# Cross-attention and a mixture of experts on one core: four dense expert pieces moved ahead of the gathered tiles, attended rows kept per batch element

## The chip, the cores and the metric

The kernel runs on one core of one Trainium2 chip. A core has TensorE (PE in the profile; PEld is its weight load), VectorE (DVE), ScalarE (ACT), GpSimd (POOL) and SyncE (SP), which issues most of the DMAs. The metric is the device time of one execution in microseconds (us).

## What is computed

```python
x = x + attn(layernorm(x), ctx, Wq, Wk, Wv, Wo)     # x (32, 56, 512), ctx (32, 1500, 512)
    # 16 query heads, 4 key/value heads of 96; keys and values from ctx and the normed x
x = x + ffn(layernorm(x), W_gate, b_gate, W_e, b_e)
    # logits = x @ W_gate + b_gate; the top 2 of 8 experts for each row
    # y_e = relu(x @ W_e + b_e); the mean of the two chosen y_e
```

There are 32 batch elements of 56 rows, so 1792 rows, which make 14 tiles of 128. Everything is float32; each product is made of three passes with operands split in a high and a low part (TERMS), so each operand is first copied ("hi") and then subtracted ("lo").

## The kernel before

Four blocks of code follow one another, `project`, `attend`, `combine` and `experts`. Each is a `with nc.Block()` with one program per engine, and at its end all engines meet: no engine begins the next block until all have ended this one.

**attend** (L538 on) loops over the 32 elements. For each one SP brings the unnormalized attended rows back, POOL divides them, and `store_att` writes them to `scratch["att"]`, a DRAM tensor of (1536 head rows, 1792 token rows): 1536 pieces of 224 bytes for an element. The rows of the first tile are read back and split by POOL at the end of this block (`first`, L650 to L654).

**combine** (L1008 on) makes the output projection, tile by tile (`output(t, parts)`, L1295: 36 matmuls of 512 columns into one bank). Tile t's attended rows are loaded by SP with `load_rows` (1536 pieces of 512 bytes), two tiles ahead, split by ACT (L1180, hi) and DVE (L1207, lo). DVE adds x and normalizes (`norm`, L926 to L938; it waits until the normed rows of the tile before have been stored, since they use one buffer), SP stores x1 and the normed rows (`store_rows`), PE turns them over (`turn`, L1279, halfway through the next tile's matmuls) and makes the logits (`logits`, L953), DVE picks the top two (`choose`), PE ranks them (`rank`), DVE finds each token's place (`put`), and POOL scatters the token numbers to `scratch["ids"]` (`scatter`, L1161, two indirect DMAs of a tile). The first 12 tiles (OS) are routed in this way: their tokens are gathered into 31 tiles (NT) by expert. The last two tiles (OD) are dense: all eight experts are computed for all their rows and weighed with 0 or a half (16 pieces, STEPS). POOL meanwhile splits the early part of the expert weights (L1149, L1154). At the end of the loop SP loads the late part of the weights of experts 0 to 3 (`load_late`, L978), then the bias (L1098, 2 MB), waits for the last scatter, loads `id_table` (L1103), and issues the late loads 4 and 5, each when POOL has split the buffer's former tenant (L1004).

**experts** (L1330 on): PE turns the id table (L1580, L1581), DVE makes the row indices (L1483 to L1489), POOL gathers rows of `scratch["xn"]` with an indirect DMA for a tile (L1434; three buffers, XRING), PE turns each (L1560), ACT and DVE split it (L1456, L1497), and PE multiplies it with its expert (`product`, L1573, 15 matmuls, banks in a ring of three). DVE adds the bias (`evict`, L1502), ACT applies the relu (L1471; L1478 with the weights of a dense piece), POOL writes the result back (`put_back`, L1424). Then come the logits of the dense tiles and the 16 dense pieces; POOL adds pieces to their rows of x1 (L1446, L1447, `summed`), and DVE closes the routed tiles in between:

```python
                    if i >= LAG and i - LAG < OS:
                        close(i - LAG)            # LAG = 3: tiles 0 to 11 behind pieces 3 to 14
```

`close(t)` (L1515, L1517) adds the two expert rows of each token, which SP has loaded with `load_y` (L1380, three buffers; the next is issued when `close` has freed one), and SP stores the tile (L1383).

Of the kernel before, what the change touches and what calls it, by code (L numbers as in the profile page):

```python
# [31 lines left out]
P = 128  # L32
# [4 lines left out]
E = 8  # L37
# [70 lines left out]

PIECES = ((0, 0, 0, 0, D), (1, 0, D, 0, D), (2, 0, 2 * D, 0, D // 2), (2, 1, 0, D // 2, D), (3, 1, D // 2, 0, D))
# [103 lines left out]
def load_rows(sp, scratch, t, att, loaded):  # L213

    sp.dma_start(att, scratch["att"].rearrange("(k p) r -> p k r", p=P)[:, :, bass.ds(t * P, P)]).then_inc(loaded, 16)
# [275 lines left out]
def attend(nc, w, stream, io, scratch):  # L491


    with ExitStack() as ctx:
# [20 lines left out]
        first = f(w["wv"][0][:]).rearrange("p k c -> p (k c)").rearrange("p (k r) -> p k r", r=P)  # L515
# [22 lines left out]
        with nc.Block() as block:  # L538
            @block.sync
            def _(sp):  # L540
# [64 lines left out]
                load_rows(sp, scratch, 0, first, first_loaded)  # L605
# [8 lines left out]
            def _(pool):  # L614
# [30 lines left out]
                for n in range(LOADS - 1):  # L645
                    split_wo(pool, stream, n)
                    if n == RAW - 1:
                        (hi, lo), third = stream["first_parts"], HT // 3
                        pool.wait_ge(first_loaded, 16)
                        pool.tensor_scalar(hi, first, 1.0, 0.0, ALU.mult, ALU.add).then_inc(stream["first_hi"], 1)  # L650
                        pool.wait_ge(stream["first_hi"], 1)
                        for i in range(3):
                            k = slice(i * third, (i + 1) * third)
                            op = pool.tensor_tensor(lo[:, k], first[:, k], f(hi[:, k]), ALU.subtract)  # L654
                        op.then_inc(stream["first_lo"], 1)
# [262 lines left out]
def norm(dve, g, t):  # L918
# [16 lines left out]
    dve.wait_ge(g["turned"], START + min(t, OS))  # L935
# [21 lines left out]
def choose(dve, g, t, sel):  # L957
# [13 lines left out]
    dve.wait_ge(g["sel_ready"], 2 * t + 2)  # L971

# [35 lines left out]
def combine(nc, stream, g, io, scratch):  # L1008

    with ExitStack() as ctx:  # L1010
# [15 lines left out]
        att = [stream["rows"], sb("att", [P, HT, P])[:]]  # L1026
        ats = [[home, sb(f"att_{n}", [P, HT, P], F32R)[:]] for home, n in zip(stream["first_parts"], ("hi", "lo"))]
        w_raw = g["area"][:, 0:2 * EARLY_W].rearrange("p (n c) -> p n c", n=2)
        home = [g["area"][0:HD, 2 * EARLY_W + i * H * Q:2 * EARLY_W + (i + 1) * H * Q] for i in range(2)]
# [6 lines left out]
        loaded = [sem(f"rows_loaded{i}") for i in range(2)]  # L1036
# [11 lines left out]

        with nc.Block() as block:
            @block.sync  # L1050
            def _(sp):
                def load(t):
                    load_rows(sp, scratch, t, att[t % 2], loaded[t % 2])
# [10 lines left out]
                load(1)  # L1064
# [11 lines left out]
                for t in range(OT):  # L1076
                    if t + 2 < OT:
# [4 lines left out]
                        if t + 2 == OT - 1:  # L1082
                            sp.wait_ge(stream["att_stored"], START + B * 16)
                        load(t + 2)
# [6 lines left out]
                    if t == OT - 2:  # L1091

                        sp.wait_ge(a_lo, START + OT - 2)
                        for e in range(LATE_RING):
                            load_late(sp, g, io, e)

                        sp.wait_ge(g["e_lo"], E)
                        sp.dma_start(g["area"][:, 0:E * D], io["be"].broadcast_to([P, E * D])).then_inc(g["bias_loaded"], 16)  # L1098
# [76 lines left out]
            def _(act):  # L1175
                def split(t):
                    act.wait_ge(loaded[t % 2], (t + t % 2) // 2 * 16)
# [14 lines left out]
                for t in range(OT - 1):  # L1192
# [3 lines left out]
                    if t < OS:  # L1196
                        turn(t)
# [4 lines left out]
            def _(dve):  # L1202
                for s in (a_lo, g["logits_ready"]):
                    dve.sem_inc(s, START)
                def split(t):
                    dve.wait_ge(a_hi, t + 1)
                    dve.tensor_tensor(ats[1][t % 2], att[t % 2], f(ats[0][t % 2]), ALU.subtract).then_inc(a_lo, 1)  # L1207
# [58 lines left out]
                find_tiles()  # L1266
                split_late_lo(dve, g, POOL_LATE)

            @block.tensor
            def _(pe):  # L1270
# [18 lines left out]
                def output(t, parts):  # L1289

                    n = 3 * HT
                    for j in range(n):
# [8 lines left out]
                        if 0 < t <= OS and j == n // 2:  # L1301
# [7 lines left out]
                    mm.then_inc(o_done, 1)  # L1309

# [19 lines left out]
def experts(nc, stream, g, io, scratch, out_d):  # L1330

    with ExitStack() as ctx:
# [15 lines left out]
        sel, half = sb("selected_dense", [P, 2, E]), sb("halves", [P, OD, E])  # L1348
# [8 lines left out]
        turned, x_hi, x_lo = sem("turned_e"), sem("xs_hi_ready"), sem("xs_lo_ready")  # L1357
# [4 lines left out]
        joined, chosen, summed = sem("joined"), sem("chosen"), sem("summed")  # L1362
# [4 lines left out]
        NV, STEPS = NT + OD, OD * E  # L1367

        with nc.Block() as block:
            @block.sync  # L1370
            def _(sp):
# [27 lines left out]
                for s in range(XRING):  # L1399
                    sp.wait_ge(y_stored[s], 16 * len(range(s, NT, XRING)))  # L1400
# [20 lines left out]
            def _(pool):  # L1421
                def put_back(j):
                    pool.wait_ge(relu_done, j + 1)
                    pool.indirect_dma_start(out=scratch["y"], out_offset=bass.IndirectOffsetOnAxis(y_row[:, j:j + 1], 0),  # L1424
                                            in_=y[:, j % XRING], in_offset=None).then_inc(y_stored[j % XRING], 16)
# [14 lines left out]

                for i in range(STEPS - 1):
                    s, rows = (NT + i) % XRING, x1[:, i // E]
                    pool.wait_ge(relu_done, NT + i + 1)
                    if i > 0:
                        pool.wait_ge(summed, i)
                    pool.tensor_tensor(rows[:, 0:D // 2], rows[:, 0:D // 2], y[:, s, 0:D // 2], ALU.add)  # L1446
# [261 lines left out]
```

## Time and profile before

| what | value |
|---|---|
| median of the runs (3 runs, 3391.44 to 3392.01) | 3391.51 us |
| the profiled execution's own time | 3390.29 us |
| its span (first to last instruction) | 3388.4 us |
| PE busy | 3341.6 us (99%) |
| DVE, ACT, POOL busy | 2052.6, 1648.8, 1051.4 us (61%, 49%, 31%) |
| mean granted TensorE clock | 0.994 |

The times of rows are microseconds from the start of the span; "mean ns" is that of one instruction. In a view of windows each engine has its busy time with the number of its instructions in brackets, then come the granted clock of TensorE (1.00 is 2.4 GHz, 0.50 is 1.2 GHz), the mean busy share of the 16 DMA engines, and GB/s. A q behind an engine's name means its sequencer; idle time stands behind an instruction in square brackets with what ended it. Matmuls overlap, so the starts of two neighbours, not the duration of one, give the pace.

### The profile page before, as it was taken

The numbers are of one execution on the slowest core, as the hardware profiler recorded it, in microseconds if no ns is written. First come the engines' busy times: TensorE is split into PE (matmuls) and PEld (weight loads), VectorE is DVE, ScalarE is ACT, GpSimd is POOL, SyncE is SP. The second block draws the span as 40 slices with busy tenths as digits, with TensorE's granted clock in tenths as the row PEclk, the third lists the DMA queues.
The fourth block names the chain that finished last, engine by engine and source line by source line (L and its number), as shares of the span: only waits on it lengthen the run. The fifth ranks groups of instructions, "written<-read, shape, count | busy, mean of one in ns | idle before, by whom it ended". The sixth has DMA issues, their size and how long they took to land. (4 is left out here: it accounts for less than half of the span.)

```text
span 3388.4 us, 64330 instructions
## 1 busy us (share of the span) xinstructions
PE 3341.6 (99%) x21610; PEld 3107.7 (92%) x21610; DVE 2052.6 (61%) x2995; ACT 1648.8 (49%) x3146; POOL 1051.4 (31%) x865
## 2 busy tenths in 40 slices
PE   8999999999999999999999999999999999998989
PEld 8989999999999999999999999999999999997777
DVE  5346666666666666666666666666666666665645
ACT  3225555555555555555555555555555555552232
POOL 0032223332333333332222222233323333326554
PEclk9999999999999999999999999999999999999989
DMA  6542222222212122222222222222222121226865
GB/s 229 198 144 59 59 65 65 65 61 61 63 46 60 56 63 65 64 65 64 65 65 59 65 57 60 65 65 65 61 61 61 47 61 55 63 75 164 195 194 188
DMA packets 307512, 282.96 MB, mean 84 GB/s; under 512 B 200634, under 2 KB 257546, under 8 KB 307338
## 3 DMA queue, kind: packets, MB, share of 16 engines
q1 hardware_dynamic: 301738, 266.10, 27.6%
q0 software_dynamic: 5728, 16.27, 1.5%
q8 instruction: 26, 0.43, 0.1%
q14 instruction: 20, 0.16, 0.0%
HBM read 208.33 MB, written 73.96 MB: 83 GB/s over the span
## 5 line engine op out<-in xcount | busy, mean ns | idle before, releaser
L822 PE MATMUL ps_proj<-wv_hi,parts 128*125 128x384 f32 x3072 | 875.6, 339 | 0.0
L767 DVE TENSOR_TENSOR probs_lo<-probs,probs_hi 125x448 fp32r<-125x448 f32 (+1 forms) x896 | 682.0, 778 | 275.7 <-ACT probs_hi L694 263.2
L809 PE MATMUL ps_proj<-parts,wk_hi 128*128 128x500 f32 x2304 | 711.1, 390 | 2.9 <-DVEq L722 2.9
L822 PEld LDWEIGHTS ps_proj<-wv_hi,parts 128*125 128x125 f32 x3072 | 560.0, 185 | 5.8
L147 POOL TENSOR_SCALAR parts<-raw 128x1000 fp32r<-128x1000 f32 (+1 forms) x198 | 238.3, 1204 | 957.2 <-PE ps_proj L822 777.8
L686 ACT ACTIVATE probs<-ps_scores 125x448 f32<-125x448 f32 (+1 forms) x896 | 463.0, 517 | 121.6 <-PE ps_scores L870 78.8
L822 PE MATMUL ps_proj<-wv_lo,parts 128*125 128x384 f32 x1536 | 518.4, 338 | 0.0
L809 PEld LDWEIGHTS ps_proj<-parts,wk_hi 128*128 128x128 f32 x2304 | 431.4, 188 | 91.6 <-DVEq L722 3.2
L673 ACT CAST values_hi<-ps_proj 125x384 fp32r<-125x384 f32 x384 | 184.4, 480 | 645.3 <-PE ps_proj L822 645.3
L694 ACT CAST probs_hi<-probs 125x448 fp32r<-125x448 f32 (+1 forms) x896 | 484.1, 540 | 28.3
L736 DVE TENSOR_TENSOR values_lo<-ps_proj,values_hi 125x384 fp32r<-125x384 f32 x384 | 214.3, 558 | 431.6 <-ACT values_hi L673 428.9
L870 PE MATMUL ps_scores<-queries_hi,keys_lo 104*125 104x224 f32 (+1 forms) x1664 | 454.6, 273 | 0.0
L865 PE MATMUL ps_scores<-queries_hi,keys_hi 96*125 96x224 f32 (+1 forms) x1664 | 452.3, 272 | 0.0
L866 PE MATMUL ps_scores<-queries_lo,keys_hi 96*125 96x224 f32 (+1 forms) x1664 | 451.8, 272 | 0.0
L888 PE MATMUL ps_attended<-probs_hi,values_hi 125*97 125x224 f32 x1664 | 447.5, 269 | 2.0 <-DVE probs_lo L767 1.6
L809 PE MATMUL ps_proj<-parts,wk_lo 128*128 128x500 f32 x1152 | 448.5, 389 | 0.0
L889 PE MATMUL ps_attended<-probs_hi,values_lo 125*96 125x224 f32 x1664 | 442.6, 266 | 0.0
L890 PE MATMUL ps_attended<-probs_lo,values_hi 125*97 125x224 f32 x1664 | 442.3, 266 | 0.0
L202 POOL TENSOR_TENSOR probs<-probs 96x448 f32<-96x448 f32 x31 | 35.7, 1152 | 1209.7 <-DMA probs<-inverse_sums 1209.7
L667 ACT CAST keys_hi<-ps_proj 96x500 fp32r<-96x500 f32 x288 | 164.9, 573 | 501.6 <-PE ps_proj L809 501.6
L727 DVE TENSOR_TENSOR keys_lo<-ps_proj,keys_hi 96x500 fp32r<-96x500 f32 x288 | 192.8, 670 | 336.6 <-ACT keys_hi L667 336.2
L870 PEld LDWEIGHTS ps_scores<-queries_hi,keys_lo 104*125 104x125 f32 (+1 forms) x1664 | 306.5, 184 | 2.3
(218 smaller groups left out, 5822.7 us busy)
## 6 DMA issues: line engine op xcount, KB each, us to landing
raw<-in_ctx SPq DMA_DIRECT2D x192, 500.0 KB, 3.6
qk_hi<-proj_out_hi SPq DMA_DIRECT2D x60, 224.0 KB, 2.0
qk_lo<-proj_out_lo SPq DMA_DIRECT2D x60, 224.0 KB, 2.4
queries_hi<-qk_hi SPq DMA_DIRECT2D x32, 336.0 KB, 3.5
queries_lo<-qk_lo SPq DMA_DIRECT2D x32, 336.0 KB, 3.6
att_raw<-attended SPq DMA_DIRECT2D x128, 84.0 KB
probs<-att_raw SPq DMA_DIRECT2D x31, 336.0 KB, 5.7
probs<-inverse_sums SPq DMA_DIRECT2D x31, 336.0 KB, 3.0
```

The source lines that it names most:

```text
L147: pool.tensor_scalar(hi, raw, 1.0, 0.0, ALU.mult, ALU.add).then_inc(stream["hi"], 1)
L686: act.activation(pr[0:R, u % PRING, 0:N], psc[0:R, u % SBANKS, 0:N], ACT.Exp, scale=SCALE).then_inc(exp_done, 1)
L694: act.copy(prs[0][0:R, u % PRING, 0:N], pr[0:R, u % PRING, 0:N]).then_inc(p_hi, 1)
L767: dve.tensor_tensor(prs[1][0:R, u % PRING, 0:N], pr[0:R, u % PRING, 0:N], f(prs[0][0:R, u % PRING, 0:N]), ALU.subtract).then_inc(p_lo, 1)
L809: mm = pe.matmul(pproj[n % 2][:, 0:CS], w["wk"][a][:, j // 3, i * P:(i + 1) * P], ct[v][:, c, j // 3, :], start=(j == 0), stop=(j == 3 * K ...
L822: mm = pe.matmul(pproj[n % 2][0:VT, 0:KD], ct[a][:, t // VTC, j // 3, s], w["wv"][v][:, j // 3, :], start=(j == 0), stop=(j == 3 * KT - 1))
L865: pe.matmul(o, kt[0][:, h, s], q[0][0:HD, c], start=True, stop=False)
L866: pe.matmul(o, kt[0][:, h, s], q[1][:, c], start=False, stop=False)
L870: mm = pe.matmul(o, kt[1][:, h, s], q[0][:, c], start=False, stop=True)
L888: pe.matmul(o, vt_hi[:, t, h], hi, start=(t == 0), stop=False)
L889: pe.matmul(pav[0:HD, h % 2, 0:GQ], vt_lo[:, t, h], hi, start=False, stop=False)
L890: mm = pe.matmul(o, vt_hi[:, t, h], lo, start=False, stop=(t == NVT))
```

## The change

It does two things, and moves steps that hang on them.

**Attended rows per element.** `scratch["att"]` becomes (32, 96, 896): `store_att` writes an element as it is, and `load_element` reads one as 128 runs of 2688 bytes. A ring of six element buffers (ERING) takes the place of two tile buffers; the rows of Wo are put in the matching order before the launch. Since 128 is no multiple of 56, a tile's split becomes one instruction for each of the three or four elements that it touches (`segments`), on ACT, DVE and, for the first tile, POOL. The late weight loads now wait for the split of the last tile, and the bias load goes in front of them.

**Four dense pieces first.** The first dense tile (12) is turned in tile 13's matmuls, at five sixths, and its logits follow the last matmul of combine; ACT and DVE split it into slot 2 of `xs`, and `shares` makes its weights, all in combine. In experts PE begins with pieces 0 to 3 of that tile; the id table is turned (`find_rows`) behind piece 0, the first gathered tile in front of piece 3. ACT's and DVE's splits of the late weights 4 to 7 are interleaved with the relu (`weigh`) and eviction of these pieces. POOL adds the four pieces (`gather_dense`) between the gathers of tiles 2 and 3. Twelve dense pieces remain behind the gathered tiles, and the 12 closes are spread over pieces 3 to 11 of them.

```diff
-    sp.dma_start(scratch["att"].rearrange("(h d) (b q) -> b d h q", d=HD, q=Q)[b],
-                 home[0].rearrange("d (h q) -> d h q", q=Q)).then_inc(stream["att_stored"], 16)
+    sp.dma_start(scratch["att"][b], home[0]).then_inc(stream["att_stored"], 16)
...
+def load_element(sp, scratch, e, home, loaded):
+    rows = scratch["att"][e].rearrange("d c -> (d c)").rearrange("(p c) -> p c", p=P)
+    sp.dma_start(home, rows).then_inc(loaded, 16)
...
+                        for e in range(ERING + 2, B):
+                            if last_tile(e - ERING) == t:
...
+                                load(e)
...
-                        sp.wait_ge(a_lo, START + OT - 2)
+                        sp.wait_ge(g["e_lo"], E)
+                        sp.dma_start(g["area"][:, 0:E * D], io["be"].broadcast_to([P, E * D])).then_inc(g["bias_loaded"], 16)
+
+                        sp.wait_ge(a_lo, START + OT - 1)
                         for e in range(LATE_RING):
                             load_late(sp, g, io, e)
...
-                    act.copy(ats[0][t % 2], att[t % 2]).then_inc(a_hi, 1)
+                    for e, q, n, c in segments(t):
+                        op = act.copy(ats[0][t % 2][:, :, c:c + n], rows_of(t, e, q, n))
+                    op.then_inc(a_hi, 1)
...
-                        if 0 < t <= OS and j == n // 2:
+                        if 0 < t and j == (n // 2 if t <= OS else 5 * n // 6):
                             turn(t - 1)
...
+                    if t == OT - 1:
+                        logits(pe, g, OS)
...
+                    if j == XRING - 1:
+                        for n in range(FIRST):
+                            gather_dense(n)
...
+                pe.wait_ge(x_lo, 1)
+                for n in range(FIRST):
+                    late_lo_done(pe, g, n)
+                    if n == FIRST - 1:
+                        turn(0)
+                    product(n, FIRST_SLOT, slice(n, n + 1))
+                    if n == 0:
+                        find_rows()
+                turn(1)
...
-                    if i >= LAG and i - LAG < OS:
-                        close(i - LAG)
+                    for t in range(closed, OS * max(i - LAG + 1, 0) // (LAST - LAG)):
+                        close(t)
+                        closed += 1
```

## Rows read from the trace of the kernel before

**Rows 1.** Windows of four stretches: us, busy by engine, clock, DMA share, GB/s.

```profile
155.00:3062.90 2907.90, 2903.01 (x19335) 2727.91 (x19333) 1803.54 (x2483) 1516.09 (x2931) 874.42 (x667) 1.00 0.23 65
3062.90:3215.50 152.60, 142.37 (x674) 115.69 (x673) 93.38 (x244) 33.33 (x44) 87.80 (x99) 0.96 0.82 192
3232.80:3238.30 5.50, 5.39 (x18) 4.51 (x18) 2.88 (x6) 0.88 (x2) 0.94 (x1) 0.53 0.43 139
3232.80:3382.50 149.70, 149.52 (x846) 127.93 (x845) 75.51 (x125) 47.02 (x81) 81.65 (x88) 0.98 0.59 194
```

**Rows 2.** Waits of TensorE over the whole span: us in total, times, longest.

```profile
PE ps_table L1580 <- DMA id_table<-token_ids: 8.6, 1, 8.6
PE ps_t L1279 <- DVE xn_g L938: 7.6, 4, 4.9
PE ps_t L1560 <- DMA x_gathered<-xn_rows,index: 5.9, 2, 5.6
```

**Rows 3.** The end of the combine block, line 1049: duration ns, start us.

```profile
L1049 SPq DRAIN  x1: 122/122/122, 3223.1 to 3223.1; - x1
...
L1049 PEldq EVENT_SEMAPHORE  x1: 51/51/51, 3223.3 to 3223.3; - x1
```

**Rows 4.** The subtractions of the late weights: duration ns min/median/max, start us.

```profile
L1004 POOL TENSOR_TENSOR parts<-raw,parts x3: 1817/1847/1854, 3211.1 to 3214.8; 128x768 fp32r<-128x768 f32 x3
```

**Rows 5.** DMA packets in 3118 to 3120 us and in 3224 to 3226 us.

```profile
DMA packets 1118, 0.62 MB, mean 312 GB/s; under 512 B 13, under 2 KB 1082, under 8 KB 1118
...
DMA packets 273, 0.75 MB, mean 373 GB/s; under 512 B 30, under 2 KB 30, under 8 KB 273
```

**Rows 6.** TensorE in order of time, behind its longest wait in this stage.

```profile
3117.03 1.12 PE L1279 MATMUL ps_t<-ident_g,xn_g 128*128 128x128 f32 x4 [4.93 <-DVE xn_g L938]
```

**Rows 7.** The chain of work that ended last: start us, us, what.

```profile
3209.81 11.98 DMA token_ids<-token_ids_f,places
...
3223.93 0.64 PE ps_table L1580 x2
...
3226.24 1.01 POOL x_gathered L1434
...
3227.56 4.10 DMA x_gathered<-xn_rows,index
...
3232.93 5.33 PE ps_e L1573 x15
3238.26 0.44 PE ps_t L1560 x4
3238.69 2.79 PE ps_o L1573 x15
...
3335.69 0.79 PE ps_g L953 x8
...
3382.54 0.70 DVE y L1502
...
3384.02 0.69 DVE x L1548
```

**Rows 8.** Groups by line, 3330 to 3389 us: busy us, mean ns.

```profile
L1446 POOL TENSOR_TENSOR x<-x,y 128x256 f32<-128x256 f32 x15 | 15.2, 1010 | 19.3 <-ACT y L1478 19.3
...
L1478 ACT ACTIVATE y<-y,halves 128x512 f32<-128x512 f32 x16 | 11.6, 724 | 34.6 <-DVE y L1502 34.6
L1447 POOL TENSOR_TENSOR x<-x,y 128x256 f32<-128x256 f32 x15 | 11.0, 734 | 0.0
...
L1517 DVE TENSOR_TENSOR raw<-raw,x_gathered 128x512 f32<-128x512 f32 x6 | 4.2, 692 | 0.2
```

**Rows 9.** DMA issues from 3040 us on: count, KB each, us to landing.

```profile
x_gathered<-expert_rows SPq DMA_DIRECT2D x8, 512.0 KB, 4.9
...
out<-raw SPq DMA_DIRECT2D x9, 256.0 KB, 4.7
raw_then_bias<-in_be SPq DMA_DIRECT2D x1, 2048.0 KB, 18.2
```

More of the change, by code:

```diff
@@ L604, in _ @@
                 sp.wait_ge(att_stored, START + (B - 1) * 16)
-                load_rows(sp, scratch, 0, first, first_loaded)
+                for e, *_ in segments(0):
+                    load_element(sp, scratch, e, first[e], first_loaded)
                 load_wo(sp, stream, io, RAW)
@@ L933, in norm @@
     dve.wait_ge(g["rstd_done"], t + 1)
[L935 removed]
+    dve.wait_ge(g["turned"], START + t)
     if t > 0:
@@ L1034, in combine @@
         pcnt = g["ptab"][:, 0:E]
-        loaded = [sem(f"rows_loaded{i}") for i in range(2)]
+        loaded, fourth_loaded = [sem(f"element_loaded{i}") for i in range(ERING)], sem("fourth_loaded")
         small_loaded, consts = g["small_loaded"], sem("consts_g")
@@ L1051, in _, with load @@
             def _(sp):
-                def load(t):
-                    load_rows(sp, scratch, t, att[t % 2], loaded[t % 2])
+                def load(e):
+                    load_element(sp, scratch, e, slots[e % ERING], loaded[e % ERING])
                 def load_x(t):
@@ L1195, in _ @@
                         split(t + 2)
-                    if t < OS:
-                        turn(t)
+                    turn(t)
+                act.copy(g["xs"][0][:, FIRST_SLOT], pt[:]).then_inc(g["x_hi"], 1)
                 for e in range(LATE_RING):
@@ L1367, in experts @@
         NV, STEPS = NT + OD, OD * E
+        LAST = STEPS - FIRST
+        dense = [(n // E, n % E) for n in range(STEPS)]
+        step = lambda n: n if n < FIRST else NT + n
+        stored = lambda s, j: 16 * len([i for i in range(j) if (FIRST + i) % XRING == s])
         with nc.Block() as block:
@@ L1439, in _ @@
                     put_back(j)
[L1441 to L1446, printed above, removed]
-                    pool.tensor_tensor(rows[:, D // 2:], rows[:, D // 2:], y[:, s, D // 2:], ALU.add).then_inc(summed, 1)
+                for n in range(FIRST, STEPS - 1):
+                    gather_dense(n)
             @block.scalar
@@ L1502, in evict, with evict_dense @@
                     dve.tensor_tensor(y[:, s], po[s][:], which, ALU.add).then_inc(biased, 1)
-                def gate(d):
-                    choose(dve, g, OS + d, sel)
-                    dve.tensor_tensor(half[:, d], sel[:, 0], sel[:, 1], ALU.add).then_inc(joined, 1)
-                    dve.wait_ge(joined, d + 1)
-                    dve.tensor_scalar(half[:, d], half[:, d], 0.5, None, ALU.mult).then_inc(chosen, 1)
+                def evict_dense(n):
+                    i = step(n)
+                    if i >= FIRST + NT and i - XRING < FIRST + NT:
+                        dve.wait_ge(y_stored[i % XRING], stored(i % XRING, NT))
+                    elif n >= XRING:
+                        dve.wait_ge(summed, n - XRING + 1)
+                    evict(i, bias[:, dense[n][1]])
                 def close(t):
@@ L1589, in _ @@
                     e = pe.value_load(expert_i[0:1, j:j + 1], min_val=0, max_val=E - 1)
-                    product(j, j, bass.ds(e, 1))
+                    pe.wait_ge(x_lo, j + 2)
+                    product(FIRST + j, j % XRING, bass.ds(e, 1))
                     if j + 2 < NV:
                         turn(j + 2)
-                logits(pe, g, OS)
-                for i in range(STEPS):
-                    product(NT + i, NT + i // E, slice(i % E, i % E + 1))
-                    if i == 0:
+                for n in range(FIRST, STEPS):
+                    v = NT + dense[n][0]
+                    pe.wait_ge(x_lo, v + 2)
+                    product(step(n), v % XRING, slice(dense[n][1], dense[n][1] + 1))
+                    if n == FIRST:
                         logits(pe, g, OS + 1)
```

208 lines of the change are left out of this document (129 added, 79 removed).

## The prediction

> **What bounds the kernel now.** I read the windows first. In attend TensorE is busy for 2903.0 of 2907.9 us at the full clock, with the DMA engines at 0.23 of their time [rows 1]: nothing that the change does to a store there can shorten it. So everything happens in the last 326 us. Combine takes 152.6 us for 142.4 us of TensorE work, with the DMAs at 0.82; experts is full from 3232.8 us on. The waits of TensorE name what is left: 7.6 us in four waits for the normed rows, 8.6 us for the id table and 5.9 us for the gathered rows [rows 2]. The last two are one hole between the blocks. The chain says how it comes about: the last scatter takes 11.98 us to land, then the id table is loaded and turned at 3223.93 us, POOL starts a gather at 3226.24 us, its rows come with the transfer that begins at 3227.56 us and takes 4.10 us, and the first product runs 5.33 us where the next takes 2.79 us [rows 7], because the clock stands at 0.53, near the 1.2 GHz level, over that stretch [rows 1].
>
> One row decides how much of this hole four dense pieces can fill: SP leaves combine at 3223.1 us, and TensorE is let into the next block at 3223.3 us [rows 3]. The pieces stand in experts, behind that meeting. They can't use the time from 3215.5 us on, only what comes after 3223.4 us.
>
> **The middle, step by step (before's clock times, combine unchanged so far).** TensorE comes out of 8 us of idleness, so piece 0 is a slow product: 5.33 us [rows 7], 3223.5 to 3228.8 us. Only then is the id table turned. From that turn to POOL's first gather before were 2.3 us (3223.93 to 3226.24), and from there to the rows 5.4 us (3226.24 to 3231.66) [rows 7]. Now: gather begins at about 3231.2 us, rows by 3236.6 us at the latest. Meanwhile TensorE does pieces 1 and 2 at 2.8 us each, to about 3235.3 us, and wants to turn gathered tile 0. The wait is between 0 and 1.3 us; the 5.4 us are those of a gather with another behind it, so I take 0.5 us. Piece 3 and a turn (2.8 and 0.44 us) bring it to 3239.5 us. The splits of tile 0 stand on ACT and DVE behind the relu and eviction of piece 2, each step some 0.7 us [rows 7, 8], and come out near 3239.7 us. I let the first gathered product begin at 3240.0 us.
>
> Before, 46 products, 31 turns and two logits stood behind 3238.26 us and took 144.2 us, to 3382.45 us. Now 43 products, 31 turns and one logits stand behind 3240.0 us: 144.2 - 3 x 2.80 - 0.79 = 135.0 us [rows 7], so 3375.0 us.
>
> **A new wait behind POOL.** The four additions are queued in front of gather 3. Piece 3 ends near 3239.1 us; evicted (0.7), weighed (0.72) and added (1.01 + 0.73) [rows 7, 8], with the splits of tiles 0 and 1 in the same two queues (about 1 us more), POOL is free at 3243.3 us. Gather 3 lands 4.1 to 5.4 us later, 3247.4 to 3248.7 us. TensorE has finished two gathered products and a turn at 3246.0 us. It waits 1.4 to 2.7 us; I take 2.0. Later gathers have three products of lead and catch up. TensorE would then end at 3377.0 us, 5.4 us earlier than before.
>
> **The meeting itself moves a little.** The bias (2 MB, landing after 18.2 us behind the first late weights [rows 9]) now stands in front of those weights, and they wait for tile 13's split as well. The bytes are the same and start at the same point, so the last of them lands near 3222 us as before, but this is now a weight: ACT has to copy it and DVE or POOL to subtract, 1.84 us on POOL [rows 4], which ends near 3224 us. The scatter, which no longer has the bias behind it but small pieces, may come sooner; that doesn't help when the weights are last. Bounds 0 and 3.6 us (if the weights came only behind all 18.2 us of the bias); I take 0.9 us, since the total of bytes decides. The turn of tile 12 (0.44 us) and the logits (0.79 us) moved into combine end at some 3217 us and hide in the same hole.
>
> **The tail gets longer.** Before, the last close is done while the last piece runs: TensorE ends at 3382.45, eviction at 3382.54, the last addition at 3384.02 to 3384.71 us [rows 7], 2.3 us behind TensorE. Now 12 closes stand behind 9 pieces, two of them behind the last eviction. That alone is 2 x 1.4 us. But the loads of the pairs bind too: the buffer of close t is refilled for close t + 3, with 4.9 us to landing [rows 9] and up to 0.5 us for SP, which also waits at t = 1, 2 and 3 for a store of 4.7 us [rows 9] in front of the next load. I laid the steps out with e3, the end of piece 3 of the twelve, as zero and 2.81 us a piece: close 3 ends at 9.2, close 7 at 19.6, close 8 at 21.7, close 9 at 23.8, close 10 at 26.2, close 11 (its load issued at 21.8 behind close 8) at 28.3, and the last addition at 29.0 us. TensorE has ended at 22.5 us. So 6.5 us stand behind TensorE in place of 2.3 us: 4.2 us lost, and TensorE isn't held up, since eviction 9 is late but only a thirteenth piece would need its bank. Bounds: 1.3 us (loads never late) and about 8 us (landing a us later).
>
> **Combine.** Bytes stay the same, packets change. 13 loads of 1536 runs of 512 bytes become runs of 2688 bytes. In a stretch that is nearly all 512-byte packets the engines moved 312 GB/s, in one with large ones 373 GB/s [rows 5]. A tile of 0.79 MB is 2.5 us against 2.1 us. With the last element's store (1536 pieces of 224 bytes) some 6 to 7 us of DMA time go, out of 0.82 x 152.6 = 125 us. The normed rows queue behind these loads, and TensorE's four waits are waits for such a store, one of 4.9 us and three that share 2.7 us [rows 2]. If each store comes 1 to 2 us sooner, those three go and the long one keeps about 3 us: 4.5 us gained. The bounds are 0 and 7.6 us plus what the clock costs after the long wait: four transposes behind it took 1.12 us where four take 0.44 us [rows 6, 7], and if the slow stretch costs what it costs the first product (5.33 - 2.79 us), it is 10 us. I take 4.5 us. On the cost side the splits become three or four instructions. ACT is busy 33 of 152.6 us and DVE 93 of 152.6 us [rows 1]; at a few tenths more for a tile this is hidden by the 10.9 us of a tile (152.6 / 14), and would cost those tenths x 13, 5 us, if DVE were the bound.
>
> The Trainium skill, "DMA: Bandwidth & Descriptors", section Specifications, puts the smallest transfer at line rate at 512 bytes. By that rule the 13 loads gain nothing and only the 224-byte store does, and the sum would be that of the first rival below. The two stretches of this trace differ by a fifth and so speak against it, but one of them is mixed.
>
> **The sum.** Middle -5.4, meeting +0.9, tail +4.2, combine -4.5: -4.8 us. Against the profiled execution's 3390.3 us that is 3385.5 us; the median of the runs is 1.2 us above that execution, so 3386.7 us. 0.2% is 6.8 us here, about what a measurement of this kernel tells from no change.
>
> **The rivals.**
> - Packets don't matter in combine (the waits stay as they are): -0.3 us, 3391.2 us. For it: TensorE's longest wait follows the scatters, and those stay. Against: the DMAs stand at 0.82, so small savings come out larger in the queue. Chance 0.15.
> - The DMA relief clears combine: all four waits and the slow clock go, -10 us there, -10.3 us in all, 3381.2 us; with a tail at its lower bound 3378.3 us. For it: three of the four waits share 2.7 us. Chance 0.35.
> - Slower: the pair loads bind the tail. The stretch behind the gathered tiles already runs the DMAs near their limit, and 12 closes must now fit between fewer pieces. Each us by which the landing of a pair exceeds 4.9 us is paid at every third close, some 3.5 us in all. At 6.3 us the kernel is as before, from 8.2 us on it is slower by 0.2%; at 8.5 us it is 3399 us. Against: 4.9 us was measured in the very same traffic. Chance 0.07.
> - My forecast, 3384 to 3391 us: 0.43.
>
> **Chances and range.** Faster by over 0.2% (under 3384.7 us): the clearing rival and a little of my own case, 0.38. Slower: 0.07. Within 0.2%: 0.55. The range goes from 3377.5 us, the second rival with a short tail, to 3396 us, the unknown costs (meeting 3.6, tail 8) without any gain in combine.
>
> **What the profile of the changed kernel would show.** The meeting 15 to 16 us behind tile 12's last matmul; the first product behind it at half clock and 5.3 us long; the id table turned behind it; a wait of 1 to 3 us in front of the turn of gathered tile 3, released by a gather; 43 products from there without a gap; two closes and an addition behind the last eviction, with DVE waiting for loads of pairs. In combine the longest wait for the normed rows at about 3 us. I would be wrong if combine's waits grew or vanished, if the meeting moved by more than 2 us against combine's matmuls, or if the last addition stood within 3 us of TensorE's end.

## The result, and the profile after

The changed kernel takes 3404.57 us (median of 6 runs, 3398.91 to 3408.93), the kernel before, timed beside it, 3393.54 us (6 runs, 3391.44 to 3396.39). The ratio is 1.003, with a 95% interval of 1.0018 to 1.0041: slower by 0.3%, 11.0 us. The prediction said 3386.7 us and gave this side 0.07. The profiled execution took 3398.9 us, the shortest of the six, with a span of 3397.2 us.

Windows of the changed kernel over the same kinds of stretches as [rows 1]: attend, combine up to its last product, from there to the meeting, from the meeting to TensorE's end, and behind it. The columns are those of [rows 1].

```profile
155.00:3063.60 2908.60, 2901.44 (x19330) 2727.41 (x19328) 1802.75 (x2483) 1514.31 (x2931) 874.17 (x669) 1.00 0.22 65
3063.60:3217.40 153.80, 144.00 (x685) 117.25 (x685) 97.92 (x273) 33.93 (x69) 78.31 (x96) 0.95 0.83 191
3217.40:3233.10 15.70, 0.04 (x1) 0.00 (x0) 2.97 (x10) 3.32 (x4) 6.04 (x3) 0.57 0.63 166
3233.10:3386.20 153.10, 150.26 (x849) 127.96 (x849) 75.74 (x118) 48.68 (x84) 83.85 (x88) 0.99 0.56 182
3386.20:3394.60 8.40, 0.03 (x1) 0.00 (x0) 7.52 (x11) 1.94 (x3) 3.72 (x4) 0.75 0.86 330
```

Read the first column: attend is as before. In the profile of before, the meeting behind attend ended at 3064.4 us (the window of [rows 1] begins 1.5 us earlier) and combine's products at 3215.4 us, 151.0 us behind it; the meeting let TensorE go on 7.9 us later, TensorE ended 159.1 us behind the meeting and the last addition 2.3 us behind that. Now it is 153.8, 15.7, 153.1 and 8.4 us. One stretch of four is shorter, by 6.0 us; the other three are longer, by 2.8, 7.8 and 6.1 us. The stretch of 153.8 us ends with tile 12's logits, which stood in experts before; they and that tile's turn are 1.2 us of the 2.8 (0.79 and 0.44 us by the prediction's rows).

The waits of TensorE from combine on, to set against [rows 2]:

```profile
PE ps_e L1654 <- PEq L1086: 15.9, 1, 15.9
PE ps_t L1333 <- DVE xn_g L959: 8.4, 3, 7.6
PE ps_t L1642 <- DMA x_gathered<-xn_rows,index: 1.2, 1, 1.2
PE ps_o L1654 <- DVE wk_lo L1570: 1.2, 1, 1.2
```

The id table and the gathered rows are gone from the list, as intended, but the first row is a new wait of 15.9 us for the end of the block itself, and the wait for the normed rows has grown to 7.6 us in one piece. The two waits of 1.2 us are new too: one for the fourth gathered tile, one for the split of the first. The long wait stands at the same place as in [rows 6], and the four transposes behind it again run at half clock (granted 0.50 from 3115 to 3120 us). DVE, which makes the normed rows, had itself waited 9.29 us for the store of the tile before. SP had issued that store at 3100.92 us, so it took 17.3 us:

```profile
3118.82 1.11 PE L1333 MATMUL ps_t<-ident_g,xn_g 128*128 128x128 f32 x4 [7.61 <-DVE xn_g L959]
3118.22 0.55 DVE L959 TENSOR_SCALAR xn_g<-x,mv_g,rstd_g 128x512 f32<-128x512 f32 x1 [9.29 <-DMA xn_rows<-xn_g]
```

The end of the combine block (line 1086, against [rows 3]), the late weights' subtractions (against [rows 4]) and the first copy of them on ACT:

```profile
L1086 POOLq DRAIN  x1: 6237/6237/6237, 3226.7 to 3226.7; - x1
...
L1086 SPq DRAIN  x1: 123/123/123, 3228.8 to 3228.8; - x1
...
L1086 PEldq EVENT_SEMAPHORE  x1: 51/51/51, 3233.1 to 3233.1; - x1
...
L1034 POOL TENSOR_TENSOR parts<-raw,parts x3: 1793/1803/2509, 3224.9 to 3228.4; 128x768 fp32r<-128x768 f32 x3
...
3223.94 1.66 ACT L1028 CAST parts<-raw 128x768 fp32r<-128x768 f32 x2 [7.33 <-DMA raw<-in_we]
```

The late weights land only in time for a copy at 3223.94 us. POOL begins its three subtractions at 3224.85 and ends them at 3230.9 us, 14 us behind the place they had before [rows 4], and its drain closes at 3232.9 us, 2.1 us later. SP, which was the last to leave before [rows 3], is through at 3228.9 us and no longer matters. Pieces of the chain behind the meeting, against [rows 7]:

```profile
3233.39 4.56 PE ps_e L1654 x15
3237.95 0.14 PE ps_table L1662 x2
...
3248.88 3.06 PE ps_o L1654 x15
3251.94 0.45 PE ps_t L1642 x4
3252.39 3.78 DMA x_gathered<-xn_rows,index
...
3378.14 5.63 DMA x_gathered<-expert_rows
3383.86 0.70 DVE x_more L1589
...
3387.23 5.22 DMA x_rows<-expert_rows
3392.54 0.70 DVE raw L1589
```

The first gathered product comes 15.5 us behind the first piece. The last four lines are new: the chain to the end now runs through loads of pairs and closes, which ran beside TensorE before. The loads themselves, against [rows 9]:

```profile
x_gathered<-expert_rows SPq DMA_DIRECT2D x8, 512.0 KB, 5.1
...
x_rows<-expert_rows SPq DMA_DIRECT2D x4, 512.0 KB, 5.6
...
raw_then_bias<-in_be SPq DMA_DIRECT2D x1, 2048.0 KB, 19.8
```

### The profile page after: what moved, and what is told of

It is laid out like the page before. It is cut to its first block and busy times, and to the rows that moved or that the text cites. A ratio compares the mean times of both kernels' runs of the same rounds, so it can differ in the third digit from the quotient of the medians.

```text
span 3397.2 us, 64417 instructions
## 1 busy us (share of the span) xinstructions
PE 3340.0 (98%) x21614; PEld 3107.4 (91%) x21614; DVE 2058.5 (61%) x3024; ACT 1649.7 (49%) x3175; POOL 1046.8 (31%) x867
```

## The experiments

Sixteen kernels ran in four groups. The kernels of one group ran on one chip, beside the same runs of the kernel before, so ratios are compared first within a group. A single profile's stages move by up to 5 us between executions of one kernel; a stage is only read where a wait explains it. "Stage" is combine from attend's end to TensorE's last matmul in it (in kernels with the pieces in front this takes in tile 12's turn and logits, 1.2 us), "meeting" from there until TensorE is let on, "middle" from there to TensorE's end, "tail" from there to the end of the last addition.

| kernel | median us (before's) | ratio [95%] | stage | meeting | middle | tail |
|---|---|---|---|---|---|---|
| group 1: e1_layout | 3391.49 (3384.10) | 1.0025 [1.0016, 1.0034] | 151.5 | 8.6 | 157.5 | 2.3 |
| e2_pieces | 3385.67 | 1.0005 [0.9997, 1.0014] | 147.1 | 7.5 | 154.2 | 7.7 |
| e3_late_first | 3393.25 | 1.0028 [1.0019, 1.0037] | 154.0 | 7.6 | 153.2 | 8.4 |
| e4_dve_late | 3395.02 | 1.0026 [1.0016, 1.0036] | 157.8 | 7.9 | 153.7 | 8.7 |
| group 2: e5_scat_before | 3409.44 (3386.06) | 1 run | 138.9 | | | |
| e6_scat_layout | 3417.45 | 1 run | 144.7 | | | |
| e7_before_again | 3383.85 | 1 run | 146.5 | 7.3 | 158.8 | 2.3 |
| e8_after_again | 3397.11 | 1.0032 [1.0019, 1.0045] | 158.7 | 9.8 | 154.2 | 10.1 |
| group 3: e9_two_xn | 3381.84 (3386.80) | 0.9984 [0.9975, 0.9993] | 142.0 | 7.8 | 157.6 | 2.3 |
| e10_pieces_two_xn | 3383.72 | 0.9989 [0.9980, 0.9998] | 144.4 | 7.6 | 153.8 | 7.9 |
| e11_layout_two_xn | 3383.52 | 0.9988 [0.9979, 0.9998] | 141.5 | 8.3 | 159.1 | 2.3 |
| e12_four_pairs | 3382.19 | 0.9985 [0.9976, 0.9994] | 146.6 | 7.6 | 154.0 | 8.4 |
| group 4: e13_after_two_xn | 3386.53 (3383.80) | 1.0007 [0.9998, 1.0016] | 145.6 | 12.0 | 156.3 | 10.2 |
| e14_late_first_two_xn | 3383.46 | 0.9995 [0.9986, 1.0004] | 147.0 | 7.6 | 153.1 | 8.4 |
| e15_half_pairs | 3376.39 | 1 run | 141.9 | 7.5 | 154.3 | 5.6 |
| e16_two_pieces | 3381.42 | 0.9992 [0.9983, 1.0001] | 143.4 | 7.5 | 156.6 | 4.3 |

**The parts one by one (group 1).** The first kernel takes the element layout alone (stores and loads of attended rows per element, splits in segments), the second the pieces and closes alone; in both the late weights stay in front of the bias. In the first they also wait for tile 13's split, as in the changed kernel.

> The element layout alone on the kernel before: store per element, ring of six element buffers, splits by segments; late weights still in front of the bias, but waiting for tile 13's split. Theory A (packets of 512 bytes cost little, the waits for the normed rows follow from bytes and scatters): combine as long as before, within 1.5 us, waits for normed rows 7 to 9 us in all, the meeting 0 to 2 us later for the wait on tile 13; time -1 to +2 us against before. Rival B (my prediction's term: the relief is worth 4.5 us and something else in the full change ate it): waits for normed rows at 3 us or less, time -3 to -5 us.

> The four dense pieces in front and the new spread of closes, with tile loads and the late weights in front of the bias as before. Theory A (the order of bias and late weights made the meeting late): meeting within 1.5 us of before's 3223.3 us, TensorE's end about 6 us earlier than before's 3382.5, a tail of 8 us behind it; time 0 to +2 us. Rival B (the pieces themselves make the meeting late, since turn, xs and the gate of tile 12 stand in front of the late splits on ACT and DVE): meeting 5 us or more later than before, time +5 us or more.

The third and the fourth are the changed kernel with one edit each (the arguments of the bias load are left out):

```
# e3: in SP's list, at tile OT - 2
-    sp.wait_ge(g["e_lo"], E)
-    sp.dma_start(area, bias broadcast)
     sp.wait_ge(a_lo, START + OT - 1)
     for e in range(LATE_RING): load_late(sp, g, io, e)
+    sp.wait_ge(g["e_lo"], E)
+    sp.dma_start(area, bias broadcast)
# e4: the late subtractions all on DVE
-LATE_RING, LO_PIECES, POOL_LATE = 4, 4, 3
+LATE_RING, LO_PIECES, POOL_LATE = 4, 4, 0
```

> The full change with one edit: the four late weight loads are issued in front of the bias load. Theory A (order): late weights land some 7 to 8 us after their issue in place of 19.7 us, the meeting is 6 to 9 us earlier than in the full change (at 3224 to 3227 us), time 6 to 9 us less than the full change. Rival B (the wait for tile 13's split, or bytes in all, decide): the meeting moves by less than 2 us.

> The full change with all late subtractions on VectorE, none on GpSimd. Theory A (GpSimd's three subtractions of 2 us behind the last weights, and its drain, are the last steps in front of the meeting): the meeting 3 to 4 us earlier than in the full change (near 3229.5 us). Rival B (GpSimd's drain waits for the scatters or the weights anyway): less than 1 us earlier.

The layout alone costs 7.4 us, where the prediction had it gain 4.5 and both theories of the first experiment were wrong: the more pessimistic had it cost 2 us at most. The pieces alone are a wash, as expected: middle 4.9 us shorter and tail 5.4 us longer than in the profile of before. TensorE's longest wait for the normed rows, in the first kernel and in the second:

```profile
3116.57 1.11 PE L1321 MATMUL ps_t<-ident_g,xn_g 128*128 128x128 f32 x4 [5.95 <-DVE xn_g L959]
```

```profile
3143.96 0.66 PE L1294 MATMUL ps_t<-ident_g,xn_g 128*128 128x128 f32 x4 [1.79 <-DVE xn_g L941]
```

This difference holds over the profiles with one buffer for the normed rows and the scatters in their place: the longest wait was 5.8 to 7.6 us in the five with the layout and 1.7, 1.8 and 4.9 us in the three without it. So the kernel before can meet a long wait too; the layout met it each time.

The two costs account for the third kernel: 7.4 + 1.6 = 9.0 us, and it is 9.2 us over the kernel before. With the late weights first its meeting is 7.6 us, half of the changed kernel's, and ends at 3225.5 us, inside the 3224 to 3227 expected. In time it had been expected 6 to 9 us under the changed kernel. That one is 11.0 us over before in both comparisons that timed it, so by this sum the order is worth some 2 us, which no interval of this group shows. The fourth kernel's meeting ended at 3229.3 us, 3.8 us earlier than the changed kernel's and where it was expected: without the late subtractions on POOL the meeting came sooner. But TensorE's products ended 4.0 us later, with a second wait for the normed rows of 4.7 us at 3154 us, and so the meeting looks 7.8 us shorter. Its time is 10.9 us over before by the medians and 8.8 us by the ratio, so no gain shows that is clear of noise.

**The scatters (group 2).** The long waits for xn_g that end at 3116 to 3120 us (4.9 us and more) begin 7 to 8 us behind the last of four scatters of token numbers, 4 bytes each. The last two of the four, in the changed kernel:

```profile
3101.75 1.42 POOL L1204 DMA_INDIRECT token_ids<-token_ids_f,places  x1 [1.94 <-DVE places L1273]
3103.47 0.96 POOL L1204 DMA_INDIRECT token_ids<-token_ids_f,places  x1 [0.30 <-issue]
```

So the next pair of kernels holds all scatters back until the stage is over (a tile has two; the expectation counts 28 for 14 tiles, but there are 24, for the 12 routed ones). Everything behind the stage comes later for it and isn't read.

```
 for t in range(OS + 1):
     if t in EXPERT_AT: split_expert(EXPERT_AT.index(t))
-    if t > 0: scatter(t - 1)
 for e in range(POOL_LATE): split_late_lo(pool, g, e)
+for t in range(OS): scatter(t)
```

> The kernel before with the 28 scatters of token numbers held back: GpSimd issues all of them behind its last late subtraction instead of two behind each tile of the combine stage. So the meeting and all that follows comes some 30 to 40 us later (28 issues of 1.2 us), and only the combine stage up to TensorE's last matmul is read. Theory S (the 4-byte scatters are what makes the DMA engines slow for 8 to 15 us at a time, and so the store of normed rows late): the waits of TensorE for xn_g after the first two tiles fall from 7.6 us (longest 4.9) to under 1.5 us, no stretch of 5 us between 3100 and 3125 stays under 120 GB/s while transfers are queued, and the stage takes 143 to 147 us instead of 151. Theory B (the bytes queued in front of the store, whatever the scatters do): the slow stretch stays, longest wait 4 to 8 us, stage 149 to 153 us.

> The element layout alone (the first experiment) with the same 28 scatters held back, read in the combine stage alone. If theory S holds, this pair shows what the larger packets are worth without the scatters: as predicted before the run, the stage would be 3 to 5 us shorter than that of the other kernel of this pair; if the packets' size never mattered, both agree within 1.5 us. Theory B: the longest wait for xn_g stays at 5 to 7 us as in the first experiment (5.9), stage 150 to 153 us.

> The kernel before, unchanged, for a profile from the same chip and hour as the others of this call. If chip and hour make the differences between the combine stages seen so far (147 to 158 us), it lies 3 us or more from its 151.0 of the first profile; if the stage's time belongs to the kernel, within 1.5 us.

> The changed kernel, unchanged, for a profile and a time beside those of this call. From the first comparison: ratio 1.002 to 1.004. Its meeting again 14 to 16 us behind tile 12's last matmul (15.7), its last addition 7.5 to 8.5 us behind TensorE's end; combine 152 to 155 us (153.8) if the stage's time belongs to the kernel.

Windows of four stretches around these scatters, the kernel before and then the same kernel with the scatters held back; the last two columns are the DMA share and the GB/s:

```profile
3095.00:3100.00 5.00, 4.76 (x23) 3.56 (x23) 4.25 (x14) 1.66 (x2) 3.33 (x4) 1.00 0.50 59
3100.00:3105.00 5.00, 5.00 (x29) 4.26 (x27) 3.06 (x11) 0.59 (x1) 3.25 (x2) 1.00 0.71 190
3105.00:3110.00 5.00, 4.73 (x22) 3.60 (x20) 1.73 (x4) 1.66 (x2) 0.00 (x0) 1.00 1.07 162
3110.00:3115.00 5.00, 3.54 (x22) 3.17 (x23) 2.87 (x7) 0.59 (x1) 0.00 (x0) 1.00 1.16 155
```

```profile
3095.00:3100.00 5.00, 4.77 (x23) 3.55 (x23) 4.25 (x14) 1.67 (x2) 1.20 (x2) 1.00 0.28 89
3100.00:3105.00 5.00, 5.00 (x29) 4.28 (x27) 3.07 (x11) 0.59 (x1) 0.00 (x0) 1.00 1.02 355
3105.00:3110.00 5.00, 5.00 (x27) 4.16 (x25) 4.09 (x11) 1.67 (x2) 4.12 (x5) 1.00 0.62 172
3110.00:3115.00 5.00, 5.00 (x28) 4.29 (x27) 3.59 (x9) 0.59 (x1) 1.06 (x2) 1.00 0.76 278
```

With the scatters, engines that are fully occupied (1.07 and 1.16) move 162 and 155 GB/s; without them the same queue is emptied at 355 GB/s with the engines at 1.02. All waits for xn_g are gone, and the stage takes 138.9 us instead of 146.5. That is theory S, and a larger gain than it had forecast (143 to 147 us). The waits for xn_g were 4.9 us in all in the execution beside it, so they are not the whole of the 7.6 us; the edit also takes the issuing of the scatters out of POOL's queue, and the two weren't separated. With the layout the stage took 144.7 us, 5.8 us more, and not 3 to 5 us less or the same, as expected: larger packets gain nothing without the scatters either. That execution had two other waits (1.4 us for ACT's xt_g, 2.0 us for DVE's selected_sum), each with a dip of the clock behind it, which pointed to the split segments. The DMA rows of six microseconds in the slow stretch, of the changed kernel and of the kernel before:

```profile
DMA packets 129, 0.46 MB, mean 76 GB/s; under 512 B 13, under 2 KB 13, under 8 KB 129
## 3 DMA queue, kind: packets, MB, share of 16 engines
q1 hardware_dynamic: 129, 0.46, 90.8%
```

```profile
DMA packets 910, 0.96 MB, mean 160 GB/s; under 512 B 72, under 2 KB 710, under 8 KB 910
## 3 DMA queue, kind: packets, MB, share of 16 engines
q1 hardware_dynamic: 870, 0.96, 107.2%
```

A packet occupied an engine for 16 x 6 x 0.908 / 129 = 0.68 us in the one and 16 x 6 x 1.072 / 870 = 0.12 us in the other, and the larger ones moved half as much. But this pair doesn't show what the size of a packet costs: in its first profile the kernel before moved only 101 GB/s from 3110 to 3116 us, with 249 packets, and the changed kernel 132 GB/s in its second.

Of the two unchanged kernels the changed one was in time as expected (ratio 1.0032). Their stages were not those of the first profiles: before took 146.5 us here and 151.0 there, so some 4 us of any one stage are chance, or come with the chip. The changed kernel's stage of 158.7 us, its meeting of 9.8 us and its tail of 10.1 us all lay outside the ranges expected. The stage had a second long wait for xn_g, 5.1 us at 3156 us. The meeting ended at 3232.8 us, as in the first profile (3233.1); it is shorter because TensorE's last matmul in the stage came 5.6 us later there.

**A second buffer for the normed rows (group 3).** If slow transfers become a wait only because the norm of a tile must see the store of the one before, two buffers take the wait away.

```
-    if t > 0:
-        dve.wait_ge(g["xn_stored"], 16 * t)
-    dve.tensor_scalar(xn[:], x1[:, s], ...)
+    if t >= 2:
+        dve.wait_ge(g["xn_stored"][s], t // 2 * 16)
+    dve.tensor_scalar(xn[:, s], x1[:, s], ...)
...
-    sp.dma_start(rows, g["xn"][:]).then_inc(g["xn_stored"], 16)
+    sp.dma_start(rows, g["xn"][:, t % 2]).then_inc(g["xn_stored"][t % 2], 16)
...
-        empty = sb("empty_places", [BLOCKS, P])
+        empty = g["id_table"]
```

The last edit, and five small tables moved into the unused end of the bias area, make the room.

> The kernel before with two buffers for the normed rows (xn_g) in place of one, each with its own semaphore for its store, so that a tile's norm waits for the store of two tiles back; room for it comes from placing five small tables elsewhere. Theory S (scatters slow the DMA engines, and the one buffer turns that into a wait of the norm): the waits of TensorE for xn_g behind tile 3 go to under 1 us, the combine stage takes 141 to 146 us against 146.5 and 151.0 in the two profiles of the kernel before, and the ratio is 0.9975 to 0.999. Rival (the next thing late takes over: the store of x1 two tiles back or the load of x): waits of 2 us or more under another name at the same place, stage 146 to 151 us, ratio 0.9993 to 1.0005.

> The pieces alone (second experiment: layout, loads and order as before) with the two buffers of normed rows. If the gains add up: the ratio of the ninth kernel, within 0.0006 of it, since the pieces alone were 1.0005; middle 154 us from the meeting to TensorE's end, tail 7.5 to 8.5 us behind it. The rival that the earlier end of the stage meets the late weights' landing and is lost in the meeting: meeting 3 us or more longer than 7.5 us.

> The element layout alone (first experiment) with the two buffers of normed rows. Two theories of the layout's 0.25%: theory Q (its loads, lumpier and more of them in front of the store of normed rows, only lengthen the one wait): with the wait gone it equals the ninth kernel, ratio 0.9975 to 0.999 and within 0.0005 of it. Theory D (the splitting of a tile in two or three segments makes ACT and DVE later by itself): it stays 4 to 6 us behind the ninth kernel in the combine stage, as the pair without scatters showed 5.7 us, so the ratio is 0.001 to 0.0018 above the ninth's, and PE waits remain at ACT's xt_g or DVE's selected_sum.

> The tenth kernel with a fourth buffer for the pairs of expert rows (the two buffers of normed rows, free by then) and the closes spread so that the last ends one dense piece earlier. If the tail waits for the depth of the ring (three loads in flight of 5.1 us each): the last addition falls from 7.7 to 8.5 us behind TensorE's end to 2.3 to 4.5 us, ratio 0.001 to 0.0015 below the tenth's. If the tail is bound by the DMA engines' rate (350 to 400 GB/s already): loads take 6.5 us or more instead of 5.1, and the last addition stays 6 to 8 us behind, ratio within 0.0005 of the tenth's.

The ninth kernel beats both: 5.0 us under the kernel before. One wait of 0.8 us for xn_g is left in its stage, although the slow stretch is still there (columns as above):

```profile
3110.00:3115.00 5.00, 5.00 (x27) 4.17 (x26) 3.62 (x10) 2.25 (x3) 0.00 (x0) 1.00 0.98 110
```

110 GB/s at a DMA share of 0.98, and TensorE is busy for all 5.00 us. The tenth and the eleventh tell the rest: with the wait gone the pieces cost 1.9 us and the layout 1.7 us against the ninth, intervals overlapping, and the layout's stage is 141.5 us, as long as the ninth's, with no wait for xn_g. So theory Q holds, and theory D, which had the stage 4 to 6 us longer, falls. The 5.8 us of the sixth kernel, in one execution, stay unexplained. The twelfth leaves the tail where it was, as the theory of the DMA rate had it. Loads of pairs there, with four in flight:

```profile
x_gathered<-expert_rows SPq DMA_DIRECT2D x4, 512.0 KB, 5.6
x_rows<-expert_rows SPq DMA_DIRECT2D x2, 512.0 KB, 6.9
xn_g<-expert_rows SPq DMA_DIRECT2D x2, 512.0 KB, 6.9
```

**The order and the tail (group 4).** The thirteenth and the fourteenth are the changed kernel and the third one with two buffers. The fifteenth is the tenth with loads of half a pair (it leaves the second expert's share out of the result), and the sixteenth the tenth with two pieces in front:

```
# e15
-sp.dma_start(pairs[t % XRING], y_rows)
+sp.dma_start(pairs[t % XRING][:, 0:D], y_rows[:, 0:D])
# e16
-FIRST, FIRST_SLOT = 4, 2
+FIRST, FIRST_SLOT = 2, 2
```

> The changed kernel as it is, with the two buffers of normed rows. Theory O (the order costs): the late weights behind the bias land at 3222 to 3224 us whatever TensorE does, so the combine stage gets shorter (142 to 146 us and 1.2 us of logits and turn) but the meeting grows to 16 to 22 us and stands at 3229 to 3233 us of the span as before; the stage's gain is lost and the ratio stays 1.001 to 1.003. Theory N (the order costs nothing that a run can measure): ratio within 0.0005 of the next kernel.

> The changed kernel with the late weights' loads in front of the bias and the two buffers of normed rows. Theory O: meeting 7.5 to 9 us behind tile 12's products and near 3217 us of the span, ratio that of the tenth kernel (0.9989), 0.998 to 0.9995, so 0.002 or more under the thirteenth's. Theory N: both alike, near 0.999 or both near 1.002.

> The tenth kernel, with each load of a tile's pairs reduced to the first row of each pair (256 KB instead of 512) and that row added twice, so the second expert's share is left out. The count of transfers, additions and waits is the same. If the DMA engines' rate binds the tail: loads land in 3 to 4 us instead of 5.3, DVE waits for none of them, and the last addition is still 5 us or more behind only if the spread of the closes asks it (two closes of 1.4 us and the addition behind the last eviction: 4.5 to 6.5 us); the tail is 1.5 to 3.5 us shorter than 7.9. If it is the fixed time from issue to landing: waits and tail stay as they were.

> The tenth kernel with two dense pieces in front of the gathered tiles and fourteen behind, the first gathered tile turned behind the second piece. If tail and middle trade one for one: TensorE stands 4 to 6 us between the second piece and the first gathered tile, meeting to TensorE's end 157 to 159.5 us instead of 153.8, last addition 2.3 to 5 us behind it instead of 7.9, ratio within 0.0005 of the tenth's 0.9989. If the four pieces in front gained in truth: ratio 0.0005 to 0.001 above the tenth's.

The order is worth 3.1 us between the medians (3386.53 and 3383.46 us, 11 runs each; the two intervals overlap), a ratio 0.0012 lower where 0.002 or more had been expected, and the thirteenth's 1.0007 is under the 1.001 to 1.003 expected. The meeting shows it, 12.0 against 7.6 us, less than the 16 to 22 expected: the late weights did land sooner when the stage was shorter. The thirteenth's profile is of its slowest execution, 8.3 us above its median, so its middle and tail are not typical. POOL's drain ends each of the two meetings:

```profile
L1086 POOLq DRAIN  x1: 5645/5645/5645, 3218.0 to 3218.0; - x1
```

```profile
L1086 POOLq DRAIN  x1: 5963/5963/5963, 3213.7 to 3213.7; - x1
```

Half the bytes took the landing of a pair from 5.3 to 3.8 us and the tail from 7.9 to 5.6 us in its one execution, within what was expected of a bound by rate; the rest is the two closes and the addition. Two pieces in front instead of four: middle 2.8 us longer and tail 3.6 us shorter, and the ratio 0.0003 from the tenth's. What the pieces win in the middle they lose in the tail, as expected, to within what these runs can tell.

## Why the prediction was wrong

**Where TensorE can use the pieces: right.** They ran only behind the meeting. The first was slow (4.56 us, 5.33 assumed), the id table was turned behind it, the first gathered product came at 15.5 us (16.6), the wait for gather 3 was 1.2 us (2.0), and the middle gained 6.0 us in the first profile and 4.6 in the second pair (5.4 forecast). A little of this is luck: the first piece and the first gather were faster than assumed, and TensorE waited 1.2 us for the split of gathered tile 0 (0.5 us assumed), which the chain has behind ACT's and DVE's splits of late weights.

**Combine: the step that failed.** "If each store comes 1 to 2 us sooner, those three go and the long one keeps about 3 us: 4.5 us gained." The long wait grew to 7.6 us, and the layout alone costs 7.4 us in time: the sign was wrong, and the term off by 12 us, three quarters of the 15.8 us between the forecast difference (-4.8) and the measured one (+11.0). The prediction compared two stretches at 312 and 373 GB/s [rows 5] and put a price on packets from them. Neither was the stretch in which the wait arose. There the engines moved 76 to 160 GB/s at full occupation, behind the scatters, and larger packets brought no gain. The Trainium skill, "DMA: Bandwidth & Descriptors", section Specifications, has 512 bytes at line rate, which made a gain of nothing here a rival at 0.15; on that it was right against the prediction, but it didn't give the loss. This trace agrees with it where the wait is gone: the stage took 141.5 us with runs of 2688 bytes and 142.0 us with runs of 512. The scatters as the cause of the slow stretch, and the one buffer as what turned it into a wait, are shown by the fifth and the ninth kernel. That the layout costs nearly all of its 7.4 us through this wait is shown by the eleventh; a direct cost of 1 or 2 us isn't excluded. Why its loads make the wait longer isn't settled. SP issued the loads of three elements, 1.03 MB, just before the store in the changed kernel, and of one tile, 0.79 MB, in the kernel before; that and slower packets in the slow stretch both fit, and no run told them apart.

**The meeting: failed.** "The bytes are the same and start at the same point [...] since the total of bytes decides", +0.9 us. The meeting grew by 7.8 and 2.5 us in the two profiles. The landing itself was nearly right: the weights, forecast near 3222 us, were copied from 3223.94 us on. What stands behind them was mis-sized. The prediction counted one subtraction of 1.84 us on POOL, but three stand there one after another, 6.0 us, and behind them another 2.1 us until POOL's drain closes, which it left out. In time the order costs less than in the profile, 3.1 us with the wait gone and some 2 us by the sum over the first group; that a later combine takes part of it back fits this, and no run shows it by itself.

**The tail: right mechanism, mis-sized.** +4.2 us forecast, +6.1 measured (+7.8 in the second pair, +5.4 with the pieces alone). The two closes and the addition stand there; what was too small is the landing of the loads. The prediction took 4.9 us for all of them, but that is the median of the eight into one kind of buffer; the four into the other took 5.4 us in the same trace of before. In the changed kernel it was 5.1 and 5.6 us, and DVE waited for loads five times, 0.23 to 1.74 us, so that the last eviction was 3.9 us late. The slower rival named this mechanism and its place, but it did not decide: it takes the middle's gain, and the pieces alone stand at 1.0005.

**The sum.** By medians of group 1 and the first comparison: layout +7.4, pieces and tail +1.6, order some +2, together 11.0 us; the last is what remains of the total and not a measurement of its own. The upper end of the range, 3396 us, was also added up too low: a meeting of 3.6 and a tail of 8 with the middle's -5.4 make +6.2 us, 3397.7 us. The measured 3404.6 us is beyond both, since the sum and its bounds allowed combine no loss.

## What to carry to other kernels

Price a transfer from the stretch in which its wait arises, not from a calmer one, and look at what was issued just before it: here 4-byte scatters, not the packets of the loads. When an engine waits for a store to free a buffer, a second buffer is the cheaper edit than faster transfers; 2 KB a partition gave 5.0 us in the kernel before and, by the differences to it in two groups, 11.0 - 2.7 = 8.3 us in the changed one. Work moved out of a hole in front goes to the end, and it is a gain only if what ran beside it there is not bound already: count the bytes that must still move behind the last gathered tile.

## What the hardware showed that I had not expected

- Behind four scatters of 128 values of 4 bytes, issued within 7 us, the DMA engines were occupied at 0.91 to 1.16 and moved 76 to 162 GB/s for some 10 us. Without the scatters the same queue ran at 355 GB/s (engines at 1.02) and 278 GB/s (at 0.76). A store of 256 KB issued among them took 17.3 us in the changed kernel.
- The bias, 2 MB broadcast to 128 partitions, landed after 15.3 to 19.2 us behind the late weights (twelve profiles) and 15.3 to 19.8 us in front of them (four), so its place in the queue made no difference to its own landing that these show.
- POOL leaves a block 2.1 us behind its last subtraction (3230.9 and 3232.9 us), the same in four profiles.
- An addition of 128x512 on DVE took 0.69 us, also where one of POOL's began while it ran, but 1.24 and 1.11 us where POOL's was already running. POOL's own additions took 0.73 us alone and 1.03 and 1.18 us in that company (the first fence is POOL, the second DVE):

```profile
3371.07 1.03 POOL L1493 TENSOR_TENSOR x<-x,y 128x256 f32<-128x256 f32 x1 [1.09 <-ACT y L1531]
3372.07 1.18 POOL L1494 TENSOR_TENSOR x<-x,y 128x256 f32<-128x256 f32 x1
```

```profile
3370.80 0.69 DVE L1591 TENSOR_TENSOR raw<-raw,x_rows 128x512 f32<-128x512 f32 x1
3371.41 1.24 DVE L1589 TENSOR_TENSOR raw<-raw,x_gathered 128x512 f32<-128x512 f32 x1
3372.68 1.11 DVE L1591 TENSOR_TENSOR raw<-raw,x_gathered 128x512 f32<-128x512 f32 x1
```
